# Gated linear attention and an MoE block on one core: the projections of q as one group, those of k as another, and the residual behind the merged step

## What is computed

```python
q = l2norm((x @ Wq).reshape(B, T, 8, 128))
k = l2norm((x @ Wk).reshape(B, T, 8, 128))
v = (x @ Wv).reshape(B, T, 8, 128)
alpha = sigmoid(x @ Wg).reshape(B, T, 8, 128)
def step(S, qkva):                       # over the 512 tokens
    q_t, k_t, v_t, a_t = qkva
    S = a_t[..., None] * S + k_t[..., None] * v_t[:, :, None, :]
    return S, einsum('bhkv,bhk->bhv', S, q_t)
x = layernorm(x + o.reshape(B, T, 1024) @ Wo)
x = layernorm(x + ffn(x))                # linear, swiglu, 8 experts of which 4 are taken, 2 shared, linear, swiglu
```

## Time and profile before

| | before |
|---|---|
| median of 3 runs | 1853.79 us (1848.47 to 1857.78) |
| the profiled execution | 1857.98 us, its span from the first to the last instruction 1856.2 us |
| PE busy | 1725.2 us, 93% of the span |
| PEld, DVE, ACT, POOL busy | 77%, 79%, 58%, 32% |
| granted TensorE clock, mean | 0.987 of full speed |

### The profile page before, as it was taken

The page is one execution under the profiler, slowest core; times in us unless marked ns, Lnnn a source line. Parts: engine busy times, 40 slices in busy tenths (PEclk is TensorE's granted clock), DMA queues, the critical chain, the costliest instruction groups (busy, mean ns, idle before and its releaser), DMA issues.

```text
span 1856.2 us, 81900 instructions
## 1 busy us (share of the span) xinstructions
PE 1725.2 (93%) x35719; PEld 1425.5 (77%) x35719; DVE 1462.5 (79%) x3391; ACT 1077.9 (58%) x2355; POOL 600.1 (32%) x474
## 2 busy tenths in 40 slices
PE   6999999999999999999999999999789999999996
PEld 5788887878878788887878888878667777777775
DVE  4878887888888778787887888788768787878786
ACT  5665555656656655665566566555455656565553
POOL 2322222232223223222322322232234444444444
PEclk9999999999999999999999999999989999999999
DMA  7000000000000000000000000000000000000000
GB/s 211 4 10 9 4 9 4 10 4 9 10 4 9 4 9 4 9 9 4 9 4 9 4 10 9 4 9 3 3 12 13 22 20 16 24 12 24 13 17 12
DMA packets 28657, 26.99 MB, mean 15 GB/s; under 512 B 1928, under 2 KB 23696, under 8 KB 28304
## 3 DMA queue, kind: packets, MB, share of 16 engines
q1 hardware_dynamic: 28304, 21.77, 3.9%
HBM read 13.38 MB, written 4.19 MB: 9 GB/s over the span
## 4 chain that ended last, share of the span: by engine, by line
PE 77%; DVE 11%; issue 6%; ACT 4%; DMA 0%; POOL 0%; DVEq 0%; SPq 0%; POOLq 0%; ACTq 0%
PE bank L527 11%; PE bank L529 10%; PE bank L528 10%; PE bank L660 8%; PE bank L615 7%; PE bank L670 5%; PE bank L646 5%; PE bank L618 5%; PE bank L567 5%; PE bank L577 4%; PE bank L634 3%; PE bank L603 3%; ACT v_sb L979 2%; DVE v_sb L1531 2%; DVE s_sb L1528 1%
## 5 line engine op out<-in xcount | busy, mean ns | idle before, releaser
L458 POOL TENSOR_TENSOR rn_sb<-ss_sb,expo 128x8 f32<-128x8 f32 x128 | 213.4, 1668 | 783.2 <-DVE ss_sb L1287 783.2
L1242 DVE TENSOR_TENSOR qq_sb<-qq_sb,tot_sb 128x512 f32<-128x512 f32 (+1 forms) x384 | 264.2, 688 | 189.5 <-PE bank L615 150.1
L1242 DVE TENSOR_TENSOR k_sb<-k_sb,tot_sb 128x512 f32<-128x512 f32 (+1 forms) x384 | 322.8, 841 | 4.7 <-PE bank L618 4.5
L1004 ACT ACTIVATE at_sb<-diag_sb 32x256 f32<-32x256 f32 x256 | 106.0, 414 | 171.6 <-DVE diag_sb L1254 166.9
L979 ACT ACTIVATE v_sb<-bank,rn_sb 128x128 f32<-128x128 f32 x512 | 139.1, 382 | 82.0 <-PE bank L529 78.5
L615 PEld LDWEIGHTS bank<-qq_sb,k_sb 128*32 128x32 f32 x12288 | 128.6, 110 | 59.6 <-issue 44.9
L615 PE MATMUL bank<-qq_sb,k_sb 128*32 128x16 f32 x12288 | 149.7, 185 | 23.2 <-issue 21.6
L968 ACT ACTIVATE a_sb<-bank 128x512 f32<-128x512 f32 x128 | 76.3, 597 | 154.1 <-PE bank L529 145.7
L660 PE MATMUL bank<-v_sb,at_sb 128*128 128x128 f32 x1024 | 151.6, 291 | 4.4 <-DVE res L1294 2.5
L495 POOL TENSOR_TENSOR wq_lo<-v_sb,wq_hi 128x512 fp32r<-128x512 f32 x80 | 104.7, 1308 | 138.0 <-ACT wq_hi L1127 138.0
L1120 ACT ACTIVATE sq_sb<-bank 128x512 f32<-128x512 f32 x160 | 95.4, 597 | 86.2 <-PE bank L529 85.7
(11 more groups left out here) (203 smaller groups left out, 4366.2 us busy)
## 6 DMA issues: line engine op xcount, KB each, us to landing
x_nat<-in_L_attn_x_dram SPq DMA_DIRECT2D x16, 256.0 KB, 3.5
x_nat<-x_all SPq DMA_DIRECT2D x16, 256.0 KB, 2.4
out_dram<-k_sb SPq DMA_DIRECT2D x16, 256.0 KB, 2.3
ew_raw<-in_L_ffn_exp_w_dram SPq DMA_DIRECT2D x3, 512.0 KB, 5.0
qq_sb<-in_L_attn_Wq_dram SPq DMA_DIRECT2D x1, 512.0 KB, 4.1
qq_sb<-in_L_attn_Wk_dram SPq DMA_DIRECT2D x1, 512.0 KB, 6.4
k_sb<-in_L_attn_Wg_dram SPq DMA_DIRECT2D x1, 512.0 KB, 7.2
k_sb<-in_L_attn_Wv_dram SPq DMA_DIRECT2D x1, 512.0 KB
```

The lines of the kernel that those rows point to most:

```text
L458: nc.gpsimd.tensor_tensor(rn_sb[par][:, i, :, :].rearrange("p h c -> p (h c)"), ss_sb[:, i * G:(i + 1) * G], expo[:, 0:G], ALU.pow).then_i ...
L1242: return nc.vector.tensor_tensor(view, view, by, ALU.mult)
```

## The change

On PE, in slots p = 0, 1 and 2, the second projection of q moves up in front of `scores(par, P, 1)`, next to the first; the second projection of k moves up next to the first, and both now stand between the transposes of head 0 and of head 1. In slot p = 3 the two of q stand together between the two transposes, and the two of k together behind `state_updates(.., 1)`. On ACT the copies are put in the order of the projections: in slots 0 to 2 q0, q1, `take_kT` of head 0, k0, k1, `take_kT` of head 1, and only then the squares. In slot p = 3 `take_kT` 0, q0, q1, `take_kT` 1, squares of q, first states, k0, k1, squares of k. On DVE `ln_halves` of the last batch moves from level 3, behind the sums, to right behind the merged step of slot p = 1. No operation is added or removed, and no size is changed.

```diff
--- before.py
+++ after.py
@@ -733,28 +733,29 @@
                     n_x = b + 2 if p == NP - 1 else b + 1
                     if has_next and p < NP - 1:
                         project(next_p, P + 1, wq, 0)
+                        project(next_p, P + 1, wq, 1)
                     scores(par, P, 1)
                     if has_prev:
                         transposes_of_k(1 - par, P - 1, 0)
-                    if has_next:
-                        if p == NP - 1:
-
-                            pe.wait_ge(xt_evac, n_x)
-                            pe.wait_ge(x_lo, n_x)
-                            project(next_p, P + 1, wq, 0)
-                            transposes_of_k(1 - par, P - 1, 1)
+                    if has_next and p == NP - 1:
+
+                        pe.wait_ge(xt_evac, n_x)
+                        pe.wait_ge(x_lo, n_x)
+                        project(next_p, P + 1, wq, 0)
                         project(next_p, P + 1, wq, 1)
-                    if has_prev and not (has_next and p == NP - 1):
+                    if has_next and p < NP - 1:
+                        project(next_p, P + 1, wk, 2)
+                        project(next_p, P + 1, wk, 3)
+                    if has_prev:
                         transposes_of_k(1 - par, P - 1, 1)
-                    if has_next:
-                        project(next_p, P + 1, wk, 2)
-                    if has_prev:
                         state_updates(1 - par, P - 1, 0)
                     scores(par, P, 3)
                     if has_prev:
                         state_updates(1 - par, P - 1, 1)
                     if has_next:
-                        project(next_p, P + 1, wk, 3)
+                        if p == NP - 1:
+                            project(next_p, P + 1, wk, 2)
+                            project(next_p, P + 1, wk, 3)
                         sums_of_squares(P + 1, 0, n_x)
                     scores(par, P, 4)
                     if has_prev:
@@ -1055,21 +1056,24 @@
                         take_kT(P - 1, 0)
                     if has_next:
                         take_tile(1 - par, P + 1, 0)
+                        take_tile(1 - par, P + 1, 1)
+                    if has_prev and p < NP - 1:
+                        take_kT(P - 1, 0)
+                    if has_next and p < NP - 1:
+                        take_tile(1 - par, P + 1, 2)
+                        take_tile(1 - par, P + 1, 3)
                     if has_prev:
-                        take_kT(P - 1, 1 if p == NP - 1 else 0)
+                        take_kT(P - 1, 1)
                     if has_next:
                         square(1 - par, P + 1, 0)
-                        take_tile(1 - par, P + 1, 1)
-                    if has_prev and p < NP - 1:
-                        take_kT(P - 1, 1)
-                    if has_next:
                         square(1 - par, P + 1, 1)
-                        take_tile(1 - par, P + 1, 2)
-                        square(1 - par, P + 1, 2)
                     if has_prev:
                         first_states(P - 1)
                     if has_next:
-                        take_tile(1 - par, P + 1, 3)
+                        if p == NP - 1:
+                            take_tile(1 - par, P + 1, 2)
+                            take_tile(1 - par, P + 1, 3)
+                        square(1 - par, P + 1, 2)
                         square(1 - par, P + 1, 3)
                         take_gate(1 - par, P + 1)
                     spread_diagonal(par, P)
@@ -1379,6 +1383,9 @@
                     dve.wait_ge(sc_evac, P * EVACS + 2)
                     grow(par, 2, "k").then_inc(k_up, 1)
                     keep_level(2, merged(par)[:, :, 1, :])
+                    if p == 1 and not first:
+                        dve.wait_ge(av_done, b * NP * HP)
+                        ln_halves(b - 1, y3, x_rows(b - 1))
                     for j in range(3, 7):
                         if j == 6 and has_next:
                             for h in range(HP):
@@ -1404,9 +1411,6 @@
                             clamp_sums(P + 1, 0)
                         if j == 4 and has_prev:
                             states(1 - par, P - 1)
-                        if j == 3 and p == 1 and not first:
-                            dve.wait_ge(av_done, b * NP * HP)
-                            ln_halves(b - 1, y3, x_rows(b - 1))
                         if j == 3 and first and p > 0:
                             low_experts(p - 1)
                         if j == 5 and p == 1 and not first:
```

## The result

The changed kernel took 1886.98 us, the median of 4 runs (1877.9 to 1893.02), the kernel before 1854.66 (4 runs). The ratio is 1.0174, with an interval of 1.0125 to 1.0224. The way was forecast, but +32 us lies outside the range, which ended at 1881 us (+27): the loss is more than twice the 13 us that the sum gave. The profiled execution took 1887.85 us.

What follows compares the result with a forecast made beforehand. PE, busy 93% of the span, was taken as the bound, its group starts nearly the cost of the work. +20.2 (ACT) - 6.8 (residual) - 0.2 (first slot) = +13.2 us, 1867 against the median; range 1846 to 1881.

Steps and rivals of the forecast that it cites:

- Part 1: PE in slots 0 to 2: grouping projections saves 0.17 us per slot, 8 us in 47 slots; nothing taken for slot 3.
- Part 2: ACT's copies and squares queue behind head 1's transposes; sums start 0.43 us later per slot, 20.2 us in 47 slots.
- The second rival: PE's issue gaps at sums and scores 4 shrink by the new wait: -1.8 us, 1852; chance 0.2.
- The third rival: From scores 3 on, where a gap binds, a slot loses 0.6 us, not 0.43: +26 us, 1880; chance 0.12.
- Part 3: Residual moved on DVE: slot p = 1 loses its 0.45 us wait before the outputs, 6.8 us over 15 batches.
- The rule against the row: Skill's rule that instruction fetching is hidden, against issue gaps of 37.6 us in 59; by the rule the sum stands at +13.2.

Runs made afterwards that it cites:

- the mended order: Changed kernel with ACT's order altered in slots 0 to 2: squares of q before take_kT of head 1, copies of k last; 1877.06 us, ratio 1.0087.
- k in front of the sums: Changed kernel, slots 0 to 2: q placed as before the change, both projections of k in front of the sums of squares, ACT's copies following; 1840.49 us, ratio 0.9916.
- q grouped alone: Changed kernel, slots 0 to 2: q0 and q1 before the merged scores, k0 between the transposes, k1 before the sums as before the change; 1858.02 us, ratio 0.9999.
- Filling the waits: Changed kernel plus an unused 128x512 matmul before the second state updates and one before the sums, slots 0 to 2; 1878.75 us, ratio 1.0119.
- slot 3 alone: Kernel before with the residual moved and the new order in slot p = 3 only; 1849.43 us, ratio 0.9956.

## Why the prediction was wrong

**Part 1, PE's own time.** Right in kind and near in size: without waits (the mended order) the sums start at 6.69 us in the mean, and at 6.83 before, 0.14 less; worked out were 0.17. But the gain is not kept: once ACT isn't the later one, scores 4 waits for DVE's `grow`, 6 of the 7 us, and the gaps that follow are longer.

**Part 2, ACT behind the transposes.** The string and its releaser are as worked out, and so is the price, 0.43 us in the slot shown and 0.38 in the mean; up to the sums the slots lost 17.9 us where 20.2 were forecast. What the order on ACT costs in all is the difference of the mended order to the change, 1.0174 to 1.0087, 16 us (the intervals are barely apart); it was sized at 28 us of waiting on PE (0.60 by 47). The second rival, waits that swallow gaps, fits that difference: PE's issue gaps of the attention stage sum up to 54.6 us in the changed kernel and to 70.1 in the mended order, in its slowest execution (52.0 before, 39.7 with k in front of the sums). Against the kernel before they didn't shrink, so no loss was given back.

**The step that failed** is in Part 2: what stands behind the sums "follows in PE's order without a wait", "so nothing absorbs it". I read the stretch behind the sums as fixed, so that a slot's loss was its later sums and nothing else. It isn't fixed: by moving k1 away from there, the change leaves scores 3, sums and scores 4 with hardly anything between them. PE then stands still there, in waits for ACT in the changed kernel and in longer gaps in the mended order, and with these pauses come more stretches of half clock (0.978 and 0.977, before 0.987). Behind the sums the slots came out 10.9 us longer, where 7 less were due. The mended order shows it alone: no wait for ACT, sums 0.1 us early, and 16 us slower than before; with k1 back in its place ("q grouped alone") those 16 us are gone. The third rival had its direction, "where a gap binds from there on", but was sized by the later start of scores 3 alone; neither a longer gap nor the clock was in it. By the rows before I could have seen both the gap and the one projection beside it.

**The clock.** I had the mean clock in the table and no term for it. Filling the waits gives some 10 us back, net of the matmuls that fill them. How the rest of what stands behind the sums divides between gaps and clock isn't settled.

**Part 3.** The wait of 0.45 us is gone, as said, and the p = 1 slots have the 7 us. The whole kernel shows 3 (0 to 6): the forecast of 6.8 is at or over the end of what was measured.

**The rule against the row.** Taking the gaps as part of the fetching of instructions was left with an "if". The runs show: the gap of batch 3 stands behind the same instruction in three kernels whose times and orders differ, with an equal number of instructions in front of it, and 33 us of added work are free in the mended order. And the traces show a count: between 60 and 1300 us the kernel before has 66 issue gaps over 0.25 us, and 61 of them stand at the same two neighbouring places (193 and 194) when PE's instructions (matmuls, weight loads and semaphores, 72842 in all) are counted through in blocks of 256. In the changed kernel it is 54 of 66, in the mended order 65 of 78. The page of the changed kernel has an instruction queue whose packets have 16 KB each in the mean:

```profile
q8 instruction: 284, 4.65, 1.0%
```

These are PE's instructions: 72842 by 256 is 284.5, and the kernels with 282 PE instructions more (141 matmuls and their weight loads) have 285 packets. Each of the 61 gaps in the kernel before ends 2.2 to 3.0 us after the start of such a packet.

The Trainium skill, "Runtime: NRT & Kernel Launch", section "Instruction fetch mechanics", gives blocks of 16 KiB, 256 instructions, and that agrees; that their fetching is hidden does not. That the gaps come at a fixed place in 256 instructions, and a fixed time behind a packet, is shown by the count; that a gap is a block still on its way is the reading that fits all runs. No run changed the fetching itself, so that last step is argued, not shown.

**Open.** Why q as a group in front of the merged scores, with k0 between the transposes, costs 8 us against slot 3 alone. It too takes a projection from between transposes and updates, but no run took that apart. And whether two projections in front of the sums are better than one: against slot 3 alone they are 7 us faster, where the intervals just overlap.

## What to carry to other kernels

A large matmul between runs of many small ones can cost less than its own time, as it stands where PE would else be idle (33 us of it were free here): before it is moved together with its like, look at what stands idle in the small runs beside it. An engine's order of copies has to follow what releases them: a copy that waits for a late step of another engine must not stand ahead of work that is ready. And a slot's loss is not only the wait: here the pauses also brought TensorE's clock down for what came next (0.978, and 0.987 with two matmuls in the waits).

## What the runs showed of the hardware

Thirty-three microseconds more of TensorE's work left the time as it was (1.0087 and 1.0089): I hadn't thought that gaps of under 2 us could hold so much. The gaps come by count and not by data: in the kernel before, 61 of 66 stand at the same place in blocks of 256 instructions of PE. And single stretches at half clock came behind quite short pauses: in the changed kernel PE was busy for 1.95 us of the 3 us up to 293.00, and then had 3.4 us at 1.2 GHz:

```profile
290.00:293.00 3.00, 1.95 (x133) 1.54 (x131) 2.23 (x7) 1.75 (x5) 1.64 (x1) 0.99 0.02 5
```
